# A fused decoder layer: standardised tiles made a slot later, attention output projected between score halves, residual input by group

## What is computed

```
x = x + mha(x, x, x, mask)            # 16 heads of 8, softmax
x = layernorm(x) * g1 + be1
x = x + mha(x, ctx, ctx)              # 16 heads of 8, 77 keys
x = layernorm(x) * g2 + be2
x = x + relu(x @ w1 + b1) @ w2 + b2   # hidden width 512
x = layernorm(x) * g3 + be3
# second layer
q, k = elu(x), elu(ctx)
kv = k.T @ ctx ; z = 1 / (q @ sum(k) + eps)
x = layernorm(x + (q @ kv) * z) * gamma + beta
```

## Time and profile before

| | |
|---|---|
| median of 3 runs | 375.33 us (369.15 to 375.81) |
| the profiled execution | 371.56 us, its span 369.2 us |
| PE / DVE / ACT / POOL busy | 275.2 / 191.0 / 152.0 / 114.5 us |
| mean granted TensorE clock | 0.816 of full |
| share of PE in the chain that ended last | 63% |

### The profile page before, as it was taken

How to read it: one execution, slowest core, us unless ns; L and a number is a source line. 1 busy time by engine, 2 the same in 40 slices (tenths; PEclk the granted TensorE clock), 3 DMA queues, 4 the chain that set the end, 5 groups by cost and what they waited for, 6 DMA issues and landing times.

```text
span 369.2 us, 7803 instructions
## 1 busy us (share of the span) xinstructions
PE 275.2 (75%) x2804; PEld 168.5 (46%) x2804; DVE 191.0 (52%) x601; ACT 152.0 (41%) x370; POOL 114.5 (31%) x218
## 2 busy tenths in 40 slices
PE   4118669688798879787978797889887974866550
PEld 3003334354474447444645474546544642644440
DVE  5075355546556646565557656755674524353121
ACT  2003414445464355444554555465434551352220
POOL 4031110111123342325141624342334236123424
PEclk9657967989896989798978998999698966585565
DMA  2570101201210011001200120011000001000000
GB/s 89 167 214 2 57 18 53 60 10 34 58 38 20 25 53 58 17 20 51 64 20 14 52 70 19 20 37 56 19 28 25 2 4 38 14 10 0 14 0 14
DMA packets 26973, 14.43 MB, mean 39 GB/s; under 512 B 7912, under 2 KB 26040, under 8 KB 26936
## 3 DMA queue, kind: packets, MB, share of 16 engines
q1 hardware_dynamic: 25928, 13.55, 12.8%
q10 hardware_dynamic: 1008, 0.40, 0.4%
HBM read 5.33 MB, written 1.05 MB: 17 GB/s over the span
## 4 chain that ended last, share of the span: by engine, by line
PE 63%; DVE 15%; POOL 9%; issue 6%; ACT 2%; DMA 2%; SPq 2%; POOLq 0%; DVEq 0%; ACTq 0%
PE proj_ps L466 10%; PE av_ps L436 8%; PE s_ps L408 6%; PE s_ps L418 5%; PE proj_ps L500 5%; PE s_ps L402 4%; PE s_ps L383 4%; PE s_ps L375 4%; PE post_ps L456 4%; POOL rstd L988 3%; PE post_ps L447 3%; PE proj_ps L516 3%; PE post_ps L452 2%; PE proj_ps L479 2%; DVE y_n L846 2%
## 5 line engine op out<-in xcount | busy, mean ns | idle before, releaser
L630 ACT ACTIVATE probs<-s_ps 128x512 f32<-128x512 f32 (+1 forms) x128 | 72.7, 596 | 72.8 <-PE s_ps L418 71.8
L791 DVE TENSOR_REDUCE neg_max<-s_ps 128x4 f32<-128x512 f32 (+1 forms) x128 | 68.3, 575 | 22.6 <-PE s_ps L383 22.6
L986 POOL TENSOR_SCALAR var_e<-mv 128x1 f32<-128x1 f32 x32 | 7.4, 230 | 162.2 <-DVE mv L840 162.2
L516 PE MATMUL proj_ps<-id_f,y_n 128*128 128x128 f32 x32 | 11.8, 368 | 33.2 <-DVE y_n L846 30.0
L807 DVE TENSOR_TENSOR max_x<-post_ps,max_is_j 128x256 bf16<-128x256 bf16 x32 | 13.6, 424 | 42.9 <-PE post_ps L393 42.9
L375 PE MATMUL s_ps<-bias_q,id_b 128*128 128x512 bf16 x64 | 24.5, 473 | 12.0 <-DMA sq_wide<-sq_lo 6.2
L636 ACT COPY av_sb<-av_ps 128x256 f32<-128x256 f32 x32 | 11.9, 371 | 51.0 <-PE av_ps L436 50.9
L466 PE MATMUL proj_ps<-x_t,w_sb 128*128 128x256 f32 x80 | 29.8, 504 | 1.2 <-issue 1.2
L418 PE MATMUL s_ps<-max_x,unit_sel 64*128 64x256 bf16 (+1 forms) x256 | 29.1, 312 | 0.0
L846 DVE TENSOR_SCALAR y_n<-x_post,mv,rstd 128x128 f32<-128x128 f32 x32 | 11.1, 346 | 29.4 <-POOL rstd L988 29.4
L652 ACT ACTIVATE x_t<-proj_ps,col_sb 128x128 f32<-128x128 f32 x32 | 14.6, 457 | 28.2 <-PE proj_ps L516 28.2
(11 more groups left out here) (107 smaller groups left out, 526.8 us busy)
## 6 DMA issues: line engine op xcount, KB each, us to landing
xt_in<-in_x_t SPq DMA_DIRECT2D x8, 128.0 KB, 2.3
sq_wide<-sq_hi SPq DMA_DIRECT2D x32, 32.0 KB, 1.9
sq_wide<-sq_lo SPq DMA_DIRECT2D x32, 32.0 KB, 1.9
cq_wide<-cq_hi SPq DMA_DIRECT2D x32, 32.0 KB, 1.9
cq_wide<-cq_lo SPq DMA_DIRECT2D x32, 32.0 KB, 1.9
out<-o_all SPq DMA_DIRECT2D x8, 128.0 KB, 1.9
sk_rows<-sk_hi SPq DMA_DIRECT2D x14, 64.0 KB, 1.9
sk_rows<-sk_lo SPq DMA_DIRECT2D x14, 64.0 KB, 1.9
```

Of the source, the lines that this page charges most:

```text
L516: nc.tensor.transpose(bank[:, 0:S], y_n[:, int(name[2]), :], id_f[:]).then_inc(full(name), 1)
L630: nc.scalar.activation(probs[0:n, h, r, :, :, :].rearrange("p u j n -> p (u j n)"), s2_ps[r][0:n, :], ACT.Exp, scale=SCALE).then_inc(M["ex ...
L791: nc.vector.tensor_reduce(neg_max[:, b, r, RH * h:RH * (h + 1)], scores, AX_X, ALU.max, negate=True).then_inc(M["max_done"], 1)
```

## The change

- PE: times_v half 1 of `prev` comes first in a slot, ahead of the query-major half of `nxt`. The transpose of y_n (place 0) moves behind the first key-major half. The transpose of att and the projection move around the second key-major half; the projection now stands ahead of the projections of place 2 and of times_v. h01 moves from place 1 to 2, h23 from 2 to 3.
- ACT: the first exp of a half stands ahead of place 0, the copy of att ahead of both exps of the second half; e_k moves from place 0 of slot 1 to place 4 of slot 0; place 3 is now called.
- DVE: y_n of the job before is made at the head of the next slot; the residual comes ahead of place 2, the statistics ahead of the widening; y of the third norm moves from place 3 to 2; the fold of the output bias moves to the end of the first iteration.
- The transposed maximum goes into the score bank s1_ps[1] in place of post_ps, so a query-major half 0 waits for the widening before it.
- x is loaded by group (`load_x`) and POOL adds the bias by group (`first_residual`) at the head of slot 0.

```diff
-        ("yc1", TAIL, 1, 0), ("h01", TAIL, 1, 1), ("h23", TAIL, 1, 2), ("ff", TAIL, 1, 4),
+        ("yc1", TAIL, 1, 0), ("h01", TAIL, 1, 2), ("h23", TAIL, 1, 3), ("ff", TAIL, 1, 4),
...
-        nmt_ps = post_ps[:, 2, 0:S // 2].bitcast(BF16)
+        nmt_ps = s1_ps[1][:, 0:S // 2].bitcast(BF16)
...
+            def load_x(g):
+                sp.dma_start(x_all[:, bass.ds(g * G, G), :], x[bass.ds(g * G, G)].rearrange("b p d -> p b d")).then_inc(
+                    M[f"x_loaded{g % 2}"], 16)
...
-                sp.dma_start(x_all[:], x.rearrange("b p d -> p b d")).then_inc(M["xall_in"], 16)
+                load_x(0)
...  (SP, iteration, behind load_ct)
+                if on(i + 1, SELF) and i + 1 > SELF:
+                    wait_reuse(sp, M["r0_ready"], i)
+                    settle()
+                    load_x(i + 1)
...  (PE, query_major, h == 0)
+                    wait_reuse(pe, M["maxt_ready"], job)
...  (PE, transpose_max)
-                wait_reuse(pe, M["xpost_ready"], job - 2)
...  (PE, iteration)
+                    if prev:
+                        times_v(i, *prev, 1)
                     if nxt:
                         query_major(*nxt, 0)
-                    if prev:
-                        times_v(i, *prev, 1)
-                    light_work(i, k, 0)
                     if cur:
                         key_major(*cur, 0)
+                    light_work(i, k, 0)
                     if prev:
                         post_transpose_pv(*prev)
                     light_work(i, k, 1)
                     if nxt:
                         query_major(*nxt, 1)
+                    if prev:
+                        post_transpose_att(*prev)
                     if cur:
                         key_major(*cur, 1)
                     if prev:
-                        post_transpose_att(*prev)
+                        post_project(*prev)
                     light_work(i, k, 2)
                     if cur:
                         times_v(i, *cur, 0)
-                    if prev:
-                        post_project(*prev)
                     if nxt:
                         transpose_max(nxt[3])
...  (ACT, light_work)
-                if (k, u) == (1, 0) and on(i, TAIL):
+                if (k, u) == (0, 4) and on(i, TAIL):
...  (ACT, iteration)
                         copy_av(*prev)
+                    if cur:
+                        exp_bank(*cur, 0, 0)
                     light_work(i, k, 0)
                     if cur:
-                        exp_bank(*cur, 0, 0)
                         exp_bank(*cur, 0, 1)
                     light_work(i, k, 1)
-                    if cur:
-                        exp_bank(*cur, 1, 0)
                     if prev:
                         copy_att(*prev)
                     if cur:
+                        exp_bank(*cur, 1, 0)
                         exp_bank(*cur, 1, 1)
                     light_work(i, k, 2)
+                    light_work(i, k, 3)
                     light_work(i, k, 4)
...  (DVE, residual, self jobs)
+                else:
+                    dve.wait_ge(M["r0_ready"], g + 1)
...  (DVE, light_work)
-                if (k, u) == (2, 3) and on(i, TAIL):
+                if (k, u) == (2, 2) and on(i, TAIL):
...  (DVE, iteration)
-                if static(i) and i == SELF:
-                    dve.wait_ge(M["r0_ready"], 1)
                 for k in range(4):
                     cur, nxt, prev, prev_y = schedule(i, k)
+                    if prev_y:
+                        standardise(*prev_y)
                     if nxt:
                         max_bank(*nxt, 0, 0)
...
                         split_max(*nxt)
+                    if prev:
+                        residual(*prev)
                     light_work(i, k, 2)
+                    if prev:
+                        statistics(*prev)
                     if nxt:
                         widen_max(*nxt)
-                    if prev:
-                        residual(*prev)
-                        statistics(*prev)
                     light_work(i, k, 3)
-                    if prev:
-                        standardise(*prev)
                     light_work(i, k, 4)
+                if static(i) and i == NEXT:
+                    fold_out_bias()
...  (POOL)
-            nc.gpsimd.tensor_tensor(r0[:], x_all[:], out_bias[:, 0:1, :].to_broadcast([P, B, P]), ALU.add).then_inc(
-                M["r0_ready"], 1)
+            def first_residual(g):
+                pool.wait_ge(M[f"x_loaded{g % 2}"], 16 * (g // 2 + 1))
+                nc.gpsimd.tensor_tensor(r0[:, bass.ds(g * G, G), :], x_all[:, bass.ds(g * G, G), :],
+                                        out_bias[:, 0:1, :].to_broadcast([P, G, P]), ALU.add).then_inc(M["r0_ready"], 1)
...  (POOL, iteration)
+                    if k == 0 and on(i, SELF):
+                        first_residual(i - SELF)
```

More of the change, by code:

```diff
@@ L221, in decoder_layer_kernel @@
         proj_ps = [psum(f"proj_ps{n}", [P, RH * S]) for n in range(2)]
-        names = """w_first w_second w_rest cols_in rows_in ident_in mask_in xall_in xt_loaded0 xt_loaded1 ct_loaded0 ct_loaded1 ct_loaded2 ct_loaded3 cn_loaded
+        names = """w_first w_second w_rest cols_in rows_in ident_in mask_in x_loaded0 x_loaded1 xt_loaded0 xt_loaded1 ct_loaded0 ct_loaded1 ct_loaded2 ct_loaded3 cn_loaded
             stored
@@ L908, in light_work @@
                     split_lo(i, "svck", "ck", G * S, C_CKB).then_inc(read("svck"), 1)
-                    if static(i) and i == NEXT:
-                        fold_out_bias()
                 if (k, u) == (3, 1) and on(i, TAIL):
@@ L970, in _ @@
             pool.wait_ge(M["rows_in"], 16)
-            pool.wait_ge(M["xall_in"], 16)
             def row(r, n):
```

## The result

The median went from 373.35 us (four runs, 369.15 to 375.81) to **321.76 us** (four runs, 320.4 to 324.88): a ratio of 0.870, 95% interval 0.859 to 0.882. The ratio compares fast runs alone and so leaves out two of the four of before (375.33 and 375.81 us), for which reason the two medians give 0.862 instead. The profiled execution took 320.4 us, 1.4 under its median.

The account below looks back on a forecast made before the run. PE was taken as bound by waits for y_n (30.0 us) and y (14.0) and the low clock behind them. Stretches of -6.4, -0.6, -7.9, -26.6 and -7.6 took 371.56 to 322.5; predicted 324, range 311 to 343.

Parts of the forecast that it names:

- The chain is hidden: Projection to y_n transpose, 2.8 us, covered by 2.7 to 4 us of PE work; y_n and y waits go.
- The middle: Five full iterations: 141.5 us of PE work, 13.5 of new waits, 3 of low clock; 158.0, so -26.6.
- DVE's loop: Query-major half waits for DVE's widening, which depends on earlier maxima: PE waits 1.25 us an iteration.
- The e_k term: ACT's e_k in slot 0 waits 1.6 us for cn_in, delaying copy_av: 1.45 us an iteration, iterations 2 to 7.
- Rival 2: Clock still falls as the new waits come in pairs in slot 1: +17.6, about 341 us; chance 0.17.
- the price of 0.42 us: Each us of low clock costs PE 0.42 us of busy time, from two iterations of the same work.
- rival 1: The cn_in wait is covered and low clock gone: 6 x 1.45 and 3 less, 312 us; chance 0.14.
- The start: To 28.87 us: PE starts the next query-major half at 22.4, limited by the last weights; -6.4, bounds 3.3 and 8.0.
- Iteration 0: Up to 57.5 us: one y_n wait partly gone, -0.6 us.
- Iterations 1 and 2: 57.5 to 105.2 us: 7.8 idle and 3.6 of low clock to be had, new waits 3.5; -7.9.
- The end: From 289.8 us: y wait -1.85, iteration 9's y_n chain 2.9 shorter; -7.6 in all, bounds 2 and 10.
- POOL's pieces: Eight POOL additions for r, 0.6 to 0.75 us each, at the head of slot 0: taken as 0, bounds 0 and 6.

Follow-up runs that it names:

- experiment 5: Changed kernel with the transposes of y_n and ACT's scaling put back ahead of key-major half 0: 320.98 us, ratio 0.859.
- experiment 6: Changed kernel with att's transpose back behind key-major half 1 and the output projection back behind times_v: 337.48 us, ratio 0.901.
- experiment 3: Changed kernel with SP issuing the next iteration's cn_in load ahead of the cq spread: 313.64 us, ratio 0.842.
- Experiment 1: Kernel before with the start alone changed (bias fold moved, x and r by group), old slot order: 363.95 us, ratio 0.979.
- experiment 4: Changed kernel with e_k alone put back into slot 1, behind copy_av and the first exp: 319.67 us, ratio 0.858.
- experiment 7: experiment 3 with the tail's x + ff sum ahead of slot 2's maxima on DVE and some q spreads issued by ACT: 306.51 us, ratio 0.8205.
- experiment 8: experiment 7 with unread matmuls on PE at the start and in the long waits of iterations 8 and 9: 301.74 us, ratio 0.8066.
- experiment 2: Kernel before with unread matmuls on PE ahead of the transposes of y_n (slots 0 and 1) and y: 354.44 us, ratio 0.951.

## Why the prediction was right, point by point

**The chain is hidden.** Right in the result, wrong in what covers it. I listed the projections, both halves of times_v, the transposed maximum, a query-major and a key-major half. Neither the key-major half nor the early projection is needed for it: without the one (experiment 5) the waits for y_n are 12.3 us in all and the time is the same, without the other (experiment 6) they are 10.2, and none in the full iterations. The early projection is worth 15 us for another reason, the waits for max_x and y. What hides y_n is thus the slot that it now has, with either cover; that move by itself, on the kernel before, was not tried.

**The middle, 158.0 forecast and 156.58 measured.** PE's idle time was put at 13.5 and is 13.1, but its two terms do not both hold. DVE's loop was put at 1.25 us an iteration; here are the waits of the middle stretch, 93.97 to 250.55, where neg_max, x and att together are 6.5 / 5 = 1.3:

```profile
PE post_ps L456 <- ACT av_sb L645: 3.7, 4, 1.4
PE s_ps L385 <- DVE neg_max L801: 2.3, 5, 0.5
PE proj_ps L517 <- DVE x L906: 2.3, 5, 0.5
PE post_ps L461 <- DVE att L831: 1.9, 5, 0.4
```

The e_k term is mis-sized: 5 x 1.45 = 7.25 forecast, 3.7 measured. The sum agrees because 2.9 us of small gaps, which it did not have (0.6 of them for y_n, 0.2 for neg_max at another line), fill the place; that is luck. For PE's work the sum had 141.5 and 3 for low clock, 144.5, and 143.51 was measured: 0.99 means low clock in 2% of 156.58, 3.1 us, which at 0.42 each costs 1.3 and not 3. Rival 2 would have needed 0.89. And the price of 0.42 us of busy time for each us of low clock: the low time fell from 22% of 184.6 (40.6 us) to 3.1, so 37.5 x 0.42 = 15.7, against 15.3 measured.

**e_k and cn_in.** The place and the mechanism are right, the size is half of the forecast. From the end of cq_lo (138.50) to e_k (148.03) it is 9.5 us, put at 9.0; ACT waits 2.44 where I said 1.6, and PE 1.38 where my terms gave 2.2 - 1.0 = 1.2, or 1.45 with the exp. But this is the longest of the six: ACT's are 1.6 to 2.4, and PE's are 1.23, 0.60, 1.38, 1.16, 0.55 and none, 4.9 us together where I had 8.7. Taken away, it is worth 8.1 us by the medians (experiment 3), rival 1 put it at 8.7 and 3 of clock, 312 us; 313.64 was measured. In the iteration that escapes it y_n comes late: DVE waits 1.81 us for POOL's rstd, PE transposes y_n at 243.03 after a wait of 0.56, and av_sb is there by then.

**The start, -6.4 forecast, -7.0 measured.** The weights were the right limit and landed near 21.8, not at 22.4. Experiment 1, at 8.5 us in the whole, is in line with it and 1.6 us of the later stretches.

**Iteration 0, -0.6 forecast, +1.4 measured: the wrong sign in this execution.** PE's idle time did fall there (28.63 - 21.92 = 6.7 before, 5.1 after), but its busy time rose from 21.92 to 24.89 as the clock fell from 0.80 to 0.67. It would be wrong to put this down to the new order. Experiments 3 and 4 have the same order in iteration 0 and took 28.7 us at a clock of 0.74 and 27.0 at 0.88; here is the second of them, with its end behind it (columns as in the earlier trace rows):

```profile
22.58:49.54 26.96, 20.58 (x191) 9.26 (x191) 12.79 (x32) 8.55 (x20) 5.51 (x12) 0.88 0.11 30
247.95:318.10 70.15, 43.01 (x375) 29.78 (x374) 27.17 (x102) 25.16 (x59) 27.67 (x50) 0.71 0.04 13
```

The old order took 28.6 us, and 28.7 in experiment 1. So one order spreads over 3 us here by the clock of the single execution, and my 28.0 lies inside. I had priced waits there and not the clock.

**Iterations 1 and 2, -7.9 forecast, -5.6 measured.** New waits 3.5 against an idle time of 42.09 - 38.31 = 3.8: right. The miss is the clock again: I let all 3.6 us of it go, and at 0.96 only 39.86 - 38.31 = 1.55 went.

**The end, -7.6 forecast, -11.35 measured, outside my bound of 10.** Here too the clock that I left out decides. I counted shorter chains; idle time fell only from 32.5 to 29.9 us (2.5). The other 8.8 us is busy time, 46.95 to 38.14, at a clock of 0.77 instead of 0.64. This split again belongs to one execution: experiments 3, 4 and 5 took 69.9 to 70.5 us for the same stretch, at 0.66 to 0.71 (second row above), that is 8.9 to 9.5 less than before and inside the bound. The forecast chain of iteration 9, 2.9 shorter, did not come: PE waits 3.80 us for y_n there, 3.55 before, and POOL's last_norm still stands ahead of var_e, which starts at 294.89, 1.5 us behind the end of mv.

**POOL's pieces, costed at 0.** Right: each took 0.73 us at the head of slot 0 and held nothing. What DVE has beside them are the maxima, which read PSUM, and, for the last five of the eight, the statistics of x, with one input, which take there what they take elsewhere.

```profile
140.69 0.73 POOL L995 TENSOR_TENSOR r<-x_all,out_bias 128x256 f32<-128x256 f32 x1
...
140.77 0.48 DVE L872 BATCH_NORM_STATS2 st_l<-x 128x6 f32<-128x128 f32 x2
```

**What the total owes to luck.** Four of five stretches missed by 1.4 to 3.8 us and the misses cancel: 0.6 and 1.4 and 3.75 more gained, 2.0 and 2.3 less, 1.5 together. Three of the five are one omission, the clock where waits and short work alternate, and two of these, iteration 0 and the end, come out otherwise in executions of nearly the same order: in experiment 4 the two together take 97.1 us and here 98.1, shared out differently. Inside the middle, the halved e_k term and the small gaps cancel as well.

## What to carry to other kernels

A wait of the engine on the path costs itself and the clock behind it; price the two apart, and read the second from two stretches of the same work at different clocks. Where PE idles between short bursts, take a stretch's clock from several executions before forecasting or explaining with it: the same order ran iteration 0 at 0.67, 0.74 and 0.88. When a chain is hidden, look at once for the small load or copy that the next engine in line waits for, and at its place in its queue: one DMA issued ahead of the others was worth 8 us here.

## What the runs showed of the hardware that was not expected

**Useless matmuls pay.** 5 or 7 unread 128x512 matmuls in the waits for y_n of slots 0 and 1 and for y (up to 1.9 us in the full iterations) took 18 us off the kernel before (372.42 to 354.44), and 3 to 10 in the longer waits of the start and the end took 4.8 off experiment 7 (306.51 to 301.74). They cost little themselves, as PE had mostly been idle (0.7 us at the place shown under experiment 8).

**A POOL instruction over SBUF can hold a small DVE instruction to its very end, and does not always.** It was 4.43 us and 1.06 us in place of 0.17, each ending 0.03 us behind POOL's addition and copy. The Trainium skill, SBUF — State Buffer, section "SBUF: two separate sides", says that GpSimd and VectorE share a pair of ports which is "an exclusive lock, not a bandwidth split": a VectorE instruction that has two inputs in SBUF, or is in a 2-port perf mode, and a GpSimd instruction that reads SBUF block each other, and whoever starts first keeps the pair for the whole instruction. The trace agrees with the subtraction's 4.43 us, with its 0.46 us behind the 0.45 of the next, and with experiment 2, where it came first; for the cast, which has one input, it agrees if that is in such a mode, which no trace here shows. It does not agree with these rows of the kernel before, where the same cast and subtraction start inside POOL's TENSOR_SCALAR, of which each takes 0.8 us, and last 0.17 us:

```profile
128.93 1.60 POOL L1008 TENSOR_SCALAR y<-x,mv_l,rstd_l 128x128 f32<-128x128 f32 x2
129.39 0.17 DVE L798 CAST nm_parts<-neg_max 128x16 bf16<-128x16 f32 x1
129.60 0.17 DVE L800 TENSOR_TENSOR nm_parts<-neg_max,nm_parts 128x16 bf16<-128x16 f32 x1
```

In the changed kernel they meet it 0.1 us later in its course: the cast (143.39) takes 0.28 us and ends 0.03 behind the first of the two, the subtraction 0.21. What makes one POOL instruction hold DVE and another not stays open.
